# A transformer kernel's first feed-forward: from plain float32 products in two halves to rounded products in three parts, with the second attention's step list moved eight slots forward

## The reference, cut to what matters

```python
# block 2: half of the positions of each batch (by a score) go through a feed-forward
k = int(l * CAPACITY_RATIO)                      # 32 of 64
scores = jnp.einsum('bld,d->bl', x, w_r) + b_r
_, idx = jax.lax.top_k(scores, k)
x_sel = jnp.take_along_axis(x, idx[:, :, None], axis=1)
h = jax.nn.gelu(jnp.einsum('bkd,df->bkf', x_sel, w1) + b1)      # 256 -> 1024
out_sel = jnp.einsum('bkf,fd->bkd', h, w2) + b2                  # 1024 -> 256
out = jnp.zeros_like(x).at[batch_ix, idx].set(out_sel)
# block 3: grouped attention, 32 query heads of 8, 8 key heads; block 4: up, relu squared, down,
# plus one dense expert scaled by the sum of the two top gate logits, then layernorm
```

## Time and profile before

| | us |
|---|---|
| median of 3 runs | 339.98 (339.67 to 342.86) |
| the profiled execution | 341.85 |
| its span, first to last instruction | 340.1 |

### The profile page before, as it was taken

One profiled execution on the slowest core, in us unless ns is written; L12 is line 12 of the kernel. 1 busy time (PEld: TensorE's weight loads), 2 busy tenths in 40 slices (PEclk: granted clock), 3 DMA queues, 4 the chain that ended last, 5 costly groups with the idle time before them and its releaser, 6 DMA issues.

```text
span 340.1 us, 7216 instructions
## 1 busy us (share of the span) xinstructions
PE 312.5 (92%) x2178; PEld 242.9 (71%) x2178; DVE 237.7 (70%) x921; ACT 199.9 (59%) x415; POOL 181.1 (53%) x294
## 2 busy tenths in 40 slices
PE   6978999999999999999998998869899999999993
PEld 5877667767676767765587886657567678888892
DVE  7878888999999998984426256754788746661264
ACT  4648887878787778768540324465768963113210
POOL 6648565677777856576604513343342822335643
PEclk9999999999999999999999999989999999999997
DMA  7999020201010101100000000000000000000000
GB/s 200 369 368 318 3 48 2 49 1 48 3 41 8 33 18 27 26 0 4 2 0 0 2 0 0 2 0 1 2 1 2 0 2 0 3 31 15 18 31 31
DMA packets 13301, 14.51 MB, mean 43 GB/s; under 512 B 2512, under 2 KB 11984, under 8 KB 13264
## 3 DMA queue, kind: packets, MB, share of 16 engines
q1 hardware_dynamic: 12688, 13.72, 12.9%
q10 hardware_dynamic: 576, 0.33, 0.3%
HBM read 10.64 MB, written 1.05 MB: 34 GB/s over the span
## 4 chain that ended last, share of the span: by engine, by line
PE 63%; DVE 16%; issue 8%; ACT 7%; POOL 5%; POOLq 0%; DVEq 0%; ACTq 0%
PE S L421 6%; PE S L761 6%; PE O L448 5%; PE ST L432 4%; DVE masked L1283 4%; PE ST L786 4%; PE S L555 4%; PE S L637 2%; PE S L704 2%; PE PJ L681 2%; PE O L718 2%; PE O L586 2%; PE PJ L394 2%; PE PJ L384 2%; PE XB L693 2%
## 5 line engine op out<-in xcount | busy, mean ns | idle before, releaser
L1283 DVE CUSTOM_DVE_ANT_0 masked<-S,band 128x192 bf16<-128x192 f32 x256 | 80.4, 354 | 12.7 <-PE S L421 11.6
L882 ACT ACTIVATE ex<-ST 128x384 f32<-128x384 f32 x128 | 61.4, 490 | 13.5 <-PE ST L432 11.8
L1067 POOL TENSOR_SCALAR rstd<-mv 128x1 f32<-128x1 f32 x40 | 12.0, 301 | 80.0 <-DVE mv L1220 79.9
L421 PE MATMUL S<-qk 128*128 128x384 f32 x128 | 53.2, 416 | 0.2
L432 PE MATMUL ST<-qk 128*128 128x192 f32 x256 | 47.7, 269 | 2.1 <-ACT ex L882 1.8
L432 PEld LDWEIGHTS ST<-qk 128*128 128x128 f32 x256 | 44.9, 189 | 4.4 <-issue 3.4
L421 PEld LDWEIGHTS S<-qk 128*128 128x128 f32 x128 | 24.1, 188 | 17.9 <-issue 16.1
L1127 POOL TENSOR_SCALAR_AFFINE_SELECT ex<-ex 128x512 f32<-128x512 f32 x32 | 21.3, 665 | 29.0 <-ACT ex L882 28.9
L448 PE MATMUL O<-ex,v 128*32 128x192 f32 x512 | 34.1, 338 | 0.0
L1414 DVE TENSOR_REDUCE mw<-S 128x8 f32<-128x512 f32 x32 | 22.0, 686 | 14.6 <-PE S L637 14.5
L852 ACT ACTIVATE hs<-PJ,sb,byhead 128x512 fp32r<-128x512 f32 x29 | 22.6, 779 | 12.4 <-PE PJ L385 12.0
(11 more groups left out here) (204 smaller groups left out, 720.7 us busy)
## 6 DMA issues: line engine op xcount, KB each, us to landing
qk<-kp SPq DMA_DIRECT2D x48, 48.0 KB
w<-in_w SPq DMA_DIRECT2D x2, 1024.0 KB, 9.8
cx<-in_cx SPq DMA_DIRECT2D x1, 1024.0 KB, 9.0
up<-in_up SPq DMA_DIRECT2D x1, 1024.0 KB, 12.3
down<-in_down SPq DMA_DIRECT2D x1, 1024.0 KB, 11.9
out<-x SPq DMA_DIRECT2D x8, 128.0 KB, 1.7
cxT<-in_cxT SPq DMA_DIRECT2D x1, 768.0 KB, 6.0
x<-in_x SPq DMA_DIRECT2D x1, 768.0 KB, 7.7
```

The source lines that it names most:

```text
L421: mm(out, r32(qp[:, t % 2, g, b, P * c:P * c + P]), r32(mv_), start=True, stop=True).then_inc(s["pe_s"], 1)
L882: A(ex[:, (n // 2) % 4, 2 * w:2 * w + 2, :], ST[n % 2][:, 0:2 * WIN].rearrange("p (h k) -> p h k", h=2), ACT.Exp, scale=SCALE).then_inc(s[ ...
L1283: last = V.tensor_tensor_reduce(out=masked[:, n % 2, h, :], in0=S[n % 2][:, WIN * h:WIN * h + WIN], in1=band[:, c, :], scale=1.0, scalar=N ...
```

## The change

1. **Rounded products.** `ffn_up` makes three products (L384/L385's scheme, `PARTS`) for each half of the contraction, six per chunk, `ffn_down` three per chunk and 128 columns. Their parts have to be made: of the weights w1 on ACT (four copies of 128x512, slots l = 4, 6, 8, 10 of tile 7) and DVE (four subtractions, l = 6, 8, 12, 15); of w2 on ACT (l = 12, 14 and e = 12, 13) and DVE (e = 2, 3, 13, 14); of the picked rows of tiles 0 to 3 on ACT and DVE (l = 2, 3 of tile 7) and of tiles 4 to 7 with each take; of each hidden chunk right after its gelu: a rounding copy on ACT, which waits for the gelu, and a subtraction on DVE (`ffn_low`), through a ring of four buffers.
2. **Three parts.** g = 0: tiles 0 to 3 (256 columns), g = 1: tiles 4 and 5 (128), g = 2: tiles 6 and 7 (128). Up: g = 0 at e = 10 to 17, g = 1 at 18 to 21 (two chunks a slot), g = 2 at 31 to 34. Down: g = 0 at 13 to 20, g = 1 at 20 to 23, g = 2 at 33 to 36, so that a chunk goes down three slots after it came up.
3. **Scatters** of tiles 0 to 5 at e = 22, 24, 26 (two each) in banks ST[0] and ST[1], of 6 and 7 at n = -3.
4. **The second list** is merged into the first: slot n runs in slot e = n + 41, after the first list's steps. So n = -18 is at e = 23 and n = 0 at e = 41, where it was the 49th slot after e = 0. The table load (`warm`) moves from n = 2 to n = -6.
5. **Loads.** `up` and `down` of block 4 (1024 KB each) are no longer loaded at the start, but into w1's and w2's place, after e = -1 and e = 14.

```diff
-        SCATTER1 = {-15: (2,), -14: (3,), -3: (4,), -2: (5,), 4: (6, 7)}
+        SCATTER = {22: (0, 1), 24: (2, 3), 26: (4, 5)}
+        def tail_up(e):
+            if 10 <= e < 18:
+                return ((0, e - 10),)
+            if 18 <= e < 22:
+                return (1, 2 * e - 36), (1, 2 * e - 35)
+            if 31 <= e < 35:
+                return (2, 2 * e - 62), (2, 2 * e - 61)
+            return ()
+        def tail_down(e):
+            if 13 <= e < 21:
+                return ((0, e - 13),) if e < 20 else ((0, 7), (1, 0), (1, 1))
+            if 21 <= e < 24:
+                return (1, 2 * e - 40), (1, 2 * e - 39)
+            if 33 <= e < 37:
+                return (2, 2 * e - 66), (2, 2 * e - 65)
+            return ()
+        AHEAD = 41
...
+            sp.wait_ge(s["f_w1"], 4)
+            load(w1[:, :, :], a["up"].rearrange("(k p) f -> p k f", p=P), "ld_up")
+            sp.wait_ge(s["f_w2"], 4)
+            load(w2[:, :, :], a["down"].rearrange("(k p) f -> p k f", p=P), "ld_down")
...
                 if m >= 2:
                     pe.wait_ge(s["fa_up"], m - 1)
-                for k in range(2):
-                    last = mm(up_bank(f), w1[:, k, P * f:P * f + P], xsT[:, k, T * half:T * half + T], start=(k == 0), stop=(k == 1))
+                for i, (k, a, b) in enumerate(PARTS):
+                    last = mm(up_bank(f)[:, 0:width(g)], r32(w1s[:, a, k, P * f:P * f + P]), r32(x_part(g, b)[:, k, :]),
+                              start=(i == 0), stop=(i == len(PARTS) - 1))
...
+                pe.wait_ge(s["f_lo"], FC * g + f + 1)
+                for m in range(width(g) // P):
+                    for i, (a, b) in enumerate(((0, 0), (1, 0), (0, 1))):
+                        last = mm(down_bank(m if g == 0 else g + 1), r32(ffn_h(g, f, a)[:, P * m:P * m + P]), r32(w2s[:, f, b, :]),
+                                  start=(f == 0 and i == 0), stop=(f == FC - 1 and i == 2))
...
-                        pe.wait_ge(s["fa_up"], 2 * FC)
+                        pe.wait_ge(s["fa_up"], 3 * FC)
...
+                A(h_f32(g, f), up_bank(f)[:, 0:width(g)], ACT.Gelu_apprx_tanh, bias=b1[:, f:f + 1]).then_inc(s["fa_up"], 1)
+                if ring_last(g, f):
+                    act.wait_ge(*ring_last(g, f))
+                if m == 0:
+                    act.wait_ge(s["pe_st"], ALL_UNITS)
+                act.wait_ge(s["fa_up"], m + 1)
+                A(r32(ffn_h(g, f, 0)), h_f32(g, f), ACT.Copy).then_inc(s["fa_hi"], 1)
...
-                if n == 2:
+                if n == -6:
                     A(warm[:, :], ident[:, 0:1], ACT.Exp)
...
+                V.tensor_tensor(r32(ffn_h(g, f, 1)), h_f32(g, f), ffn_h(g, f, 0), ALU.subtract).then_inc(s["f_lo"], 1)
...
-            for n in SLOTS1:
+            for T_, l in SLOTS_ALL:
+                slot_(T_, l)
+                if since_end(T_, l) - AHEAD in SLOTS1:
+                    slot1(since_end(T_, l) - AHEAD)
+            for n in SLOTS1[since_end(*SLOTS_ALL[-1]) - AHEAD + 1 - SLOTS1[0]:]:
                 slot1(n)
```

More of the change, by code:

```diff
@@ L299, in pv_units, with since_end @@
             return [u for u in (place(T_, l, PV_LAG + 1), place(T_, l, PV_LAG)) if live(*u)]
[L301 to L309, removed]
+        def tail_up(e):
[14 more added lines that the diff above has]
+            return ()
+        def since_end(T_, l):
+            return UNITS * T_ + l - END
+        AHEAD = 41
         @block.sync
@@ L397, in slot_ @@
             def slot_(T_, l):
[L398 to L402, removed]
+                for g, f in tail_up(since_end(T_, l)):
+                    ffn_up(g, f)
+                for g, f in tail_down(since_end(T_, l)):
+                    ffn_down(g, f)
                 t, r = T_, l
@@ L515, in slot_ @@
                     ctx_keys(*CTX_K[UNITS * T_ + l])
-                if UNITS * T_ + l in (END + 26, END + 27):
-                    scatter(UNITS * T_ + l - END - 26)
+                for t in SCATTER.get(since_end(T_, l), ()):
+                    scatter(t)
             def ctx_keys(p, g):
@@ L828, in slot_ @@
                     nc.scalar.copy(selT(t), MT[:, 0:P])
[L829 removed]
+                    last = nc.scalar.copy(xsT[:, :, 64 * t:64 * t + 64], MT[:, P:2 * P].rearrange("p (k c) -> p k c", k=2))
+                    if t >= 4:
+                        if t == 4:
+                            act.wait_ge(s["pe_proj"], 4 * TILES)
+                        if t == 6:
+                            act.wait_ge(s["ld_kb0"], KB_DMA * (TILES - 2))
+                            act.wait_ge(s["ld_kb1"], KB_DMA * (TILES - 2))
+                        o = 64 * (t % 2)
+                        last = A(r32(x_part(t // 2 - 1, 0)[:, :, o:o + 64]), MT[:, P:2 * P].rearrange("p (k c) -> p k c", k=2), ACT.Copy)
+                    last.then_inc(s["fa_x"], 1)
                 for b in range(2):
@@ L889, in slot_ @@
                         .then_inc(s["act_mt"], 1)
-                f = tail_up(T_, l)
-                if f is not None:
-                    gelu(0, f)
+                for g, f in tail_up(since_end(T_, l)):
+                    gelu(g, f)
+                if T_ == 7 and l in (4, 6, 8, 10):
+                    i = l // 2 - 2
+                    k, c = divmod(i, 2)
+                    if i == 0:
+                        act.wait_ge(s["ld_late"], LATE)
+                    nc.scalar.copy(r32(w1s[:, 0, k, 512 * c:512 * c + 512]), w1[:, k, 512 * c:512 * c + 512]).then_inc(s["f_w1h"], 1)
+                i = {(7, 12): 0, (7, 14): 1, (8, 12): 2, (8, 13): 3}.get((T_, l))
+                if i is not None:
+                    act.wait_ge(s["pe_st"], UNITS * (TILES - 1) if i < 2 else ALL_UNITS)
+                    nc.scalar.copy(r32(w2s[:, 2 * i:2 * i + 2, 0, :]), w2[:, 2 * i:2 * i + 2, :]).then_inc(s["f_w2h"], 1)
+                if (T_, l) == (7, 2):
+                    act.wait_ge(s["fa_x"], 4)
+                    act.wait_ge(s["pe_proj"], 4 * TILES)
+                    nc.scalar.copy(r32(x_part(0, 0)), xsT[:, :, 0:T]).then_inc(s["f_xh"], 1)
                 if UNITS * T_ + l == END + 6:
@@ L1392, in ffn_add @@
                 V.tensor_tensor(x[:, t, :], scatter_bank(t), x[:, t, :], ALU.add).then_inc(s["f_x"], 1)
-            for T_, l in SLOTS_ALL:
-                slot_(T_, l)
             def slot1(n):
-                c = at(n, -4, 8, 2)
-                if c is not None:
-                    ffn_out(2 + c)
+                if n > -11:
+                    for g, f in tail_up(n + AHEAD - 1):
+                        ffn_low(g, f)
+                if n == -4:
+                    ffn_out(3)
                 t = at(n, 21, 4, TILES)
@@ L1415, in slot1 @@
                                     AX, ALU.max).then_inc(s["g_max"], 1)
-                for t in SCATTER1.get(n - 1, ()):
-                    ffn_add(t)
+                if n == -2:
+                    ffn_add(6)
+                    ffn_add(7)
                 p = at(n, -9, 8, PAIRS)
```

219 lines of the change are left out of this document (135 added, 84 removed).

## The result

The changed kernel takes 355.31 us (351.33 to 358.44, 4 runs) beside 341.42 us for the kernel before on the same chip (339.67 to 342.93). The ratio goes by its two faster runs, 351.33 and 353.52, since the other two (357.10, and 358.44, which is the profiled one) lie over 1.5% above the fastest: it is 1.0335, 95% interval [1.027, 1.0399]. Slower by 3.4%. The forecast was 343.7 us with a range of 338 to 348.5: the direction came out, the size did not, and the time lies outside the range.

The account below looks back on a forecast made before the run. PE's queue of products was taken to bound the seam from e = 10 on, apart from tile 7's short chain. Terms +1.8 + 9.0 + 1.6 - 7.1 - 1.6 = +3.7 us gave 343.7 us, range 338 to 348.5.

Parts of the forecast that it names:

- What bounds the kernel: From e = 10 on the seam is PE's queue of products, except tile 7's chain from gated product to take.
- The products as a whole: All feed-forward products on PE: 26.9 us against 27.7, so rounding saves only 0.8 us; 128-column products taken at 0.10.
- Tile 7's score slots, +1.8: Added subtractions on DVE and copies on ACT lengthen tile 7's slots by 1.8 us; slots e = 0 to 9 by 0.
- Gated product of tile 7, +9.0 late: At e = 22, more products stand ahead of it in PE's queue, 18.6 us instead of 9.1: 9.0 us late.
- From there to the take, +1.6: Gated product to e = 30: merged POOL and DVE steps lengthen tile 7's chain by 1.6 us, bounds +0.5 and +2.4.
- From the take to n = 0, -7.1: PE has less work left between take and n = 0: 14.9 us instead of 22.0, bounds 13.8 and 16.5.
- Units 0 to 4, -1.6: Second attention's first units: the wait for the last down's bias and the scatter now come ahead of n = 0, -1.6 us.
- The sum: All terms from tile 7's score slots to units 0 to 4 together: +3.7 us, giving 343.7 us.
- PE stays fed: Seam from gated product to take: PE's queue costs the same in any order, waits are saved; -2.9, 337.1 us; chance 0.22.
- Costly parts: Tile 7's subtractions stretched beside busy POOL, 128-column products at 0.12: +2.2 + 1.9, 347.8 us; chance 0.10.
- The clock falls: Waits between e = 26 and 30 bring half speed in part 2's products: 345.5 to 347.3 us; chance 0.18.

Follow-up runs that it names:

- the filled run: The changed kernel plus 18 float32 128x128 products that nothing reads, in slots e = 25 to 30 where PE waited: 351.46 us, ratio 1.0271.
- the run with AHEAD 46: The changed kernel plus 18 products that nothing reads, with the second list five slots later (AHEAD 46 instead of 41): 356.23 us, ratio 1.0405.

## Why the prediction was wrong, step by step

**What bounds the kernel.** Right. The seam is PE's queue: the same 51.0 us from tile 6's gated product to n = 4 come out in two orders.

**The products as a whole.** Right within bounds. A rounded product of 128 columns takes 0.107 to 0.118 us (12 in 1.37 us above; with full clock in the filled run, 12 from 208.98 to 210.27, 0.107, and 24 from 205.40 to 208.22, 0.118). I took 0.10, between 0.06 and 0.12, and 96 of them make 0.7 to 1.7 us of difference. The figure of the Trainium skill (TensorE: Matmul & The Clock Gate, Back-to-back issue gap), 81 ns, is not reached here: 0.107 is the least in the rows read, and the measurement decides. Rounding saved about 1 us between the gated products, where I had 0.8 for the whole seam.

**Tile 7's score slots, +1.8.** Right for the slots themselves: 17.23 us instead of 15.73, +1.5. What failed is the sentence that gives slots e = 0 to 9 nothing. From e = 0 to the gated product of tile 6 it is 10.99 us instead of 9.21, so that the whole stretch is +3.3 to +3.5. The run without parts in the changed kernel's order, cut at the same two places:

```profile
138.15:153.89 15.74, 15.14 (x138) 11.24 (x138) 13.89 (x81) 11.00 (x25) 10.60 (x20) 1.00 0.02 5
153.89:163.98 10.09, 8.88 (x86) 5.77 (x85) 3.17 (x9) 7.64 (x19) 7.79 (x14) 1.00 0.01 2
```

So the parts are 1.5 us in the slots and 0.9 behind them, 2.4 in all, and another 0.9 is the order: part 0's first chunk now stands ahead of tile 6's gated product. The parts' second share comes through tile 6's chain: POOL's normalising takes 1.75 us there instead of 1.24, and PE waits 1.70 us for tile 6's score, where it waits 0.79 without parts.

**Gated product of tile 7, +9.0 late.** Right: +9.1, and PE full in the whole stretch, 22.92 of 22.92.

**From there to the take, +1.6.** Too low: +3.6. The mechanism was the one described (POOL's deviation and DVE's normalising ahead of the score, then the rank), but I summed it as if DVE and PE were otherwise free. The adds of tiles 0 to 5 run on DVE in the same 11 us, and steps that took 0.41 and 0.35 took 1.07 and 0.74 there beside POOL's building of keys (DVE's normalising L1309 and the select L1417; the same select took 0.35 in the run with AHEAD 46, which has POOL's keys later). The run that moved the merged steps away got 1.1 us back, and by the estimate given there 2.4 us of the 3.6 are the merged steps, 0.4 the feed-forward's own and 0.7 the clock.

**From the take to n = 0, -7.1.** This is the step that failed: +1.5. At full clock the stretch is 16.7 us, 1.8 over my 14.9, and that was the second, smaller error: two waits for the spread's copy on ACT, of 1.2 and 1.0 us, that I had put at 0.8 and 0.6, and part 2's up products, 5.5 us instead of 4.8. The other 6.8 us are the clock, which the term of -7.1 took to be full throughout. I had that as a rival at 0.18, with its place right (waits of some 2 us between e = 26 and 30), and priced it by the earlier trace rows, 3.6 us of half speed for each fall. It lasted 20.5 us, and it fell on the densest products of the seam.

**Units 0 to 4, -1.6.** Right.

**The sum.** Forecast +3.7; with the two sizes right (3.5 and 3.6) and 16.7 us at full clock (22.0 before, so -5.3) it is +9.3; the filled run lies 8.8 above the 342.69 us of its group. The clock adds the other 6. Of the +9.3 another 0.7 is clock, in the chain; the 8.6 left, on the median of 339.98, make 348.6 us, at the very end of my range. So the clock is by far the largest error, but three sizes erred in the same direction beside it (1.7, 1.3 and 1.8 us too low), and they had used up the range by themselves.

**Rivals.** *PE stays fed* was wrong for this kernel, PE stood 3.7 us in the chain, but its principle is what the float32 run with part 1 later shows: with PE fed, and no parts, 341.10 us, no more and no less than before. *Costly parts* was true in part (2.4 us up to tile 6's gated product, and the stretched steps in the chain). *The clock falls* was the case. The rivals were treated as exclusive; all of them at once is what happened, and the range had no room for that.

What the change costs, then, by the ratios to the kernel before: the order alone 1.5% (no parts, the changed order), the parts of the weights alone 1.4% (in the order with part 1 later), and together with the parts of rows and gelus and the long low clock, 3.4 to 4.4%. No version here beats the kernel before; the best has part 1 later, no parts and the second list merged, and equals it.

## What to carry to other kernels

In a stretch where one engine is full, moving its work about changes nothing by itself: count first how long it stands there (3.1 us here), since that is all an order can win, and count the steps on other engines that a cheaper product needs ahead of it against what the product saves (1 us here, for 2.4 and more). Then look at where the new order leaves that engine waiting with dense work right behind: the low clock is paid on that work, and its price must be taken with a range up to the whole stretch, not from one short fall seen elsewhere. And add rivals with different places instead of choosing among them.

## What the runs showed of the hardware

- The granted clock fell to 0.50 at 200 us, where PE had small waits, and stayed there for 20.5 us, 19 of them with PE full, in both profiles of the changed kernel. With part 2's up in float32, or all products in float32, it came back after 6.8 us, but so it did with rounded products in another order. What made the long one is open.
- It can fall while PE is full: at 204 us in the run with AHEAD 46, two microseconds after PE had taken up work again behind a wait of 0.75 us.
- A fall seen in one profiled execution need not be in the timed runs: taking it away shortened the profile's stretch by 1.5 us and left the times as they were.
- Three rounded products with 256 columns take nearly as long as one in float32. PE timeline, changed kernel, part 0's down:

```profile
177.66 0.52 PE L627 MATMUL ST<-qk 128*128 128x256 f32 x3
178.02 0.52 PE L627 MATMUL PJ<-qk 128*128 128x256 f32 x3
178.38 0.38 PE L515 MATMUL XB<-ident,osb 128*128 128x128 f32 x2
```

Three rounded ones are 0.36 us by the starts, one in float32 0.43: 0.07 us saved for each, while each rounded operand asks ACT for a copy and DVE for a subtraction. The parts must be nearly free to pay, and where the columns are halved and the products doubled, nothing is left.
